# The last layer's K and V projections at the fused stage's beginning, and both masked copies of K written by VectorE

## The reference

```
qn, kn, vn = ln(query), ln(key), ln(value)          # query: L0's output; key = value: the context
Q, K, V = qn @ wq + bq, kn @ wk + bk, vn @ wv + bv   # 16 heads of 8
attn = softmax(Q K^T / sqrt(8));  x = query + (attn V) @ wo + bo
out = x + gelu(ln2(x) @ w1 + b1) @ w2 + b2           # hidden width 512
```

## Time and profile before

| | |
|---|---|
| median of 3 runs | 1389.48 us (1388.59 to 1390.74) |
| the profiled execution, first to last instruction (span) | 1387.9 us; the profile has no other time of its own, and the median stands 1.6 us above |
| mean granted TensorE clock | 0.960 |
| busy share: PE, DVE, ACT, POOL | 89%, 68%, 71%, 65% |
| fused stage, from its first instruction to the MLP's first `up` matmul | 912.2 to 1258.6 us |
| MLP | 1258.6 to the end |
| packets of hardware DMA queues | 23.5% of 16 engines' span |

### The profile page before, as it was taken

How to read it: one execution, slowest core, us unless ns; L and a number is a source line. 1 busy time by engine, 2 the same in 40 slices (tenths; PEclk the granted TensorE clock), 3 DMA queues, 4 the chain that set the end, 5 groups by cost and what they waited for, 6 DMA issues and landing times. The chain is left out here.

```text
span 1387.9 us, 59975 instructions
## 1 busy us (share of the span) xinstructions
PE 1238.4 (89%) x23094; PEld 1036.4 (75%) x23094; DVE 944.3 (68%) x2136; ACT 980.7 (71%) x1956; POOL 897.7 (65%) x1432
## 2 busy tenths in 40 slices
PE   4999999989999998958999999925889998898997
PEld 2778888777788887937999999924677776675775
DVE  3788888877887886595555555525999999864331
ACT  1677787777888887346788776614888888875553
POOL 2577777777777665216999998758677777413431
PEclk9999999999999999579999999966999999999999
DMA  4233434332222320151322222322232333112221
GB/s 126 71 111 110 121 107 127 108 94 87 84 83 83 91 69 26 35 156 39 89 84 81 81 84 66 65 73 69 76 88 82 89 89 91 59 47 61 69 68 46
DMA packets 140285, 113.96 MB, mean 82 GB/s; under 512 B 17184, under 2 KB 113952, under 8 KB 140192
## 3 DMA queue, kind: packets, MB, share of 16 engines
q1 hardware_dynamic: 131744, 95.42, 23.5%
q0 software_dynamic: 8448, 17.32, 5.0%
HBM read 78.55 MB, written 34.08 MB: 81 GB/s over the span
## 5 line engine op out<-in xcount | busy, mean ns | idle before, releaser
L912 DVE TENSOR_REDUCE at_mx<-at_ps_s 128x16 f32<-128x1024 f32 x128 | 156.1, 1220 | 90.4 <-PE at_ps_s L599 46.3
L818 ACT ACTIVATE at_pt<-at_ps_t 128x1024 f32<-128x1024 f32 x128 | 130.6, 1020 | 54.7 <-PE at_ps_t L613 54.0
L811 ACT ACTIVATE at_pr<-at_dd 128x1024 f32<-128x1024 f32 x128 | 135.2, 1056 | 34.6 <-DVE at_dd L920 34.5
L2452 DVE COPY ex_wt<-experts 128x1156 f32 x133 | 102.8, 773 | 82.3 <-DVE ex_y L2458 74.0
L2410 ACT ACTIVATE ex_hg<-ex_ps_h,ex_wt 128x128 f32<-128x128 f32 x544 | 155.1, 375 | 1.2 <-PE ex_ps_y L2369 1.2
L2338 POOL DMA_INDIRECT ex_xg<-x,ex_ti x136 | 139.0, 1022 | 23.4 <-issue 21.8
L920 DVE TENSOR_TENSOR at_dd<-at_ps_s,at_mx 128x1024 f32<-128x1024 f32 x128 | 153.7, 1202 | 0.1
L2360 PE MATMUL ex_ps_h<-ex_xt,ex_wt 128*128 128x128 f32 x1088 | 147.1, 278 | 1.0 <-ACT ex_xt L2402 0.8
L1992 POOL DMA_INDIRECT l_yg<-rows,l_sl x128 | 126.1, 985 | 31.9 <-issue 29.5
L613 PE MATMUL at_ps_t<-ident,at_pr 128*128 128x128 f32 x1024 | 139.3, 279 | 6.1 <-issue 4.2
L2369 PE MATMUL ex_ps_y<-ex_wt,ex_hg 128*128 128x128 f32 x1088 | 143.7, 275 | 0.4 <-ACT ex_hg L2410 0.4
(11 more groups left out here) (262 smaller groups left out, 3154.5 us busy)
## 6 DMA issues: line engine op xcount, KB each, us to landing
rows<-ex_y SPq DMA_DIRECT2D x136, 64.0 KB
x<-at_ln_out SPq DMA_DIRECT2D x32, 256.0 KB, 3.2
at_kx<-in_xt SPq DMA_DIRECT2D x16, 256.0 KB, 2.8
at_qx<-in_xt SPq DMA_DIRECT2D x16, 256.0 KB, 2.8
at_vin<-in_xt SPq DMA_DIRECT2D x16, 256.0 KB, 2.9
at_xr<-in_x SPq DMA_DIRECT2D x16, 256.0 KB, 3.0
cx<-in_ctx SPq DMA_DIRECT2D x16, 256.0 KB, 3.2
x1t<-at_xt SPq DMA_DIRECT2D x16, 256.0 KB, 3.3
```

What stands on the lines that cost most here:

```text
L811: act.activation(pr[:, p], dd[:, p], ACT.Exp, scale=SCALE).then_inc(p_ready, 1)
L818: act.activation(pt[:, 2 * h + p], ps_t[:, :, :, :], ACT.Copy).then_inc(pt_ready, 1)
L912: dve.tensor_reduce(mx[:, p], ps_s[:, :, 4 * p:4 * p + 4, :], AX.X, ALU.max).then_inc(mx_ready, 1)
```

## The change

The context's tile `x2t` lives until the end, and `ctxzt` and its 16 copies go. At the fused stage's beginning PE projects K and V of all 16 groups, each into one of two banks of the score tile `ps_s`. ACT copies K back over the context in `x2t` (`keep_k`); DVE copies V into parts of `pt`, `dd` and `pr` that the loop doesn't use yet (`keep_v`), and SP stores it from there to a DRAM buffer `ctxv`. In the loop PE has no K and V projections any more; SP loads one group of V per step, ACT's `copy_v` reads it from SBUF, and DVE's new `mask_k` writes both masked copies from the kept K, just behind `front_moments`. The 22 matmuls go. The MLP's `hid` and `y` take the place of `dd`.

```diff
 # SP
-                def load_k(a): ...
+                def store_v(g):
+                    sp.wait_ge(vt_ready, g + 1)
+                    sp.dma_start(layer.kv_src[:, bass.ts(g, GT)], staged(g)).then_inc(v_out, 16)
                 def load_v(a):
+                    if a.unrolled and a.g == 0:
+                        sp.wait_ge(v_out, 16 * NG)
                     if beyond(a.g, 0):
-                        sp.wait_ge(v_ready, a.g)
+                        sp.wait_ge(vx_ready, a.g)
 # SP, step: behind load_front
+                    if a.unrolled and -3 <= a.g < 0:
+                        for g in ((0, 1, 2, 3, 4), (5, 6, 7, 8, 9, 10), (11, 12, 13, 14, 15))[a.g + 3]:
+                            store_v(g)
 # PE
+                def project_k(g):
+                    if g > 1:
+                        pe.wait_ge(kt_ready, g - 1)
+                    pe.matmul(bank[g % 2][:, :], layer.wk[:, :], zt[:, bass.ts(g, GT)], ...).then_inc(early_k, 1)
+                def project_v(g):
+                    if g > 1:
+                        pe.wait_ge(vt_ready, g - 1)
+                    ... 16 matmuls into bank[2 + g % 2] as before ...
+                    mm.then_inc(early_v, 1)
 # PE, step
-                        project_k(a.shift(1))
-                        project_v(a)
 # PE, before the steps
-                for k in range(22):
-                    pe.matmul(spare[:, 0:P], c.ident[:, :], c.num[:, 0:P], start=True, stop=True)
+                for g in range(NG):
+                    project_k(g)
+                    project_v(g)
 # ACT
-                def mask_k(a): ... two activations ps_g -> kb ...
+                def keep_k(g):
+                    act.wait_ge(early_k, g + 1)
+                    act.wait_ge(early_v, g + 1)
+                    act.activation(zt[:, bass.ts(g, GT)], bank[g % 2][:, :], ACT.Copy).then_inc(kt_ready, 1)
 # ACT, step: first thing
+                    if a.unrolled and -2 <= g < 0:
+                        for e in ((0, 1, 2, 3, 4, 5, 6, 7), (8, 9, 10, 11, 12, 13, 14, 15))[g + 2]:
+                            keep_k(e)
 # DVE
+                def keep_v(g):
+                    dve.wait_ge(early_v, g + 1)
+                    dve.tensor_copy(staged(g), bank[2 + g % 2][:, :]).then_inc(vt_ready, 1)
+                def mask_k(a):
+                    if a.unrolled and a.g == 0:
+                        dve.wait_ge(kt_ready, NG)
+                        dve.wait_ge(side_ready, 1)
+                    if beyond(a.g, 0):
+                        dve.wait_ge(s_ready, 2 * a.g)
+                    for j in range(2):
+                        ins = dve.tensor_scalar(kb[:, j, :], zt[:, bass.ts(a.place, GT)], c.side[:, 2 + j:3 + j],
+                                                side[:, 0, 2 + j:3 + j], ALU.mult, ALU.add)
+                    ins.then_inc(kb_ready, 1)
 # DVE, step: first thing
+                    if a.unrolled and -3 <= g < -1:
+                        for e in ((0, 1, 2, 3, 4), (9, 10))[g + 3]:
+                            keep_v(e)
 # DVE, step: between front_moments and maximum(2g+2, 0)
+                    if a.shift(1).exists():
+                        mask_k(a.shift(1))
+                    if a.unrolled and -3 <= g < -1:
+                        for e in ((5, 6, 7, 8), (11, 12, 13, 14, 15))[g + 3]:
+                            keep_v(e)
+                    if a.unrolled and g == -1:
+                        dve.wait_ge(v_out, 16 * NG)
 # attention_phase, route_phase, expert_phase
-  ctxzt: 5 + 11 copies x2t -> ctxzt, and the waits for them
```

More of the change, by code:

```diff
@@ L1469, in fused_phase @@
         z4t_ready, qx_ready = n.sem("z4t_ready"), n.sem("qx_ready")
-        in_k, in_v = n.sem("in_k"), n.sem("in_v")
+        in_v, v_out = n.sem("in_v"), n.sem("v_out")
+        early_k, early_v = n.sem("early_k"), n.sem("early_v")
+        kt_ready, vt_ready = n.sem("kt_ready"), n.sem("vt_ready")
         tok_out = [n.sem(f"tok_out{i}") for i in range(2)]
@@ L1481, in fused_phase, with staged @@
         xb_ready, y_ready = n.sem("xb_ready"), n.sem("y_ready")
+        zt = layer.out_tr
+        bank = [ps_s[:, i].rearrange("p a b -> p (a b)") for i in range(4)]
+        def staged(g):
+            whole = (pt.rearrange("p h b r q -> p (h b r q)") if g < NG // 2 else
+                     dd.rearrange("p u r b s -> p (u r b s)") if g < 3 * NG // 4 else
+                     pr.rearrange("p u r b s -> p (u r b s)"))
+            return whole[:, bass.ts(g if g < NG // 2 else g % 4, GT)]
         def held(a):
@@ L1494, in _, with load_v @@
             def _(sp):
[L1495 to L1502 removed]
+                def store_v(g):
+                    sp.wait_ge(vt_ready, g + 1)
+                    sp.dma_start(layer.kv_src[:, bass.ts(g, GT)], staged(g)).then_inc(v_out, 16)
+                def load_v(a):
+                    if a.unrolled and a.g == 0:
+                        sp.wait_ge(v_out, 16 * NG)
+                    if beyond(a.g, 0):
+                        sp.wait_ge(vx_ready, a.g)
                     sp.dma_start(vin[:, :], layer.kv_src[:, bass.ts(a.place, GT)]).then_inc(in_v, 16)
@@ L1541, in scores @@
                         pe.wait_ge(d_ready, 2 * quad)
+                    else:
+                        pe.wait_ge(kt_ready, NG)
+                        pe.wait_ge(vt_ready, NG)
                     for b in range(QB):
@@ L1596, in widen @@
                               stop=True).then_inc(r_ready, 1)
[L1598 to L1601, removed]
+                def project_k(g):
+                    if g > 1:
+                        pe.wait_ge(kt_ready, g - 1)
+                    pe.matmul(bank[g % 2][:, :], layer.wk[:, :], zt[:, bass.ts(g, GT)], start=True, stop=True).then_inc(
+                        early_k, 1)
                 def project_q(a):
@@ L1613, in project_v @@
                         for j in range(2):
-                            mm = pe.matmul(ps_g[64 * j:64 * j + 64, t:t + SEQ], vin[:, t:t + SEQ],
-                                           w[:, :, j, :], start=True, stop=True)
-                    mm.then_inc(v_ready, 1)
+                            mm = pe.matmul(bank[2 + g % 2][64 * j:64 * j + 64, t:t + SEQ],
+                                           zt[:, GT * g + t:GT * g + t + SEQ], w[:, :, j, :], start=True, stop=True)
+                    mm.then_inc(early_v, 1)
                 def project_out(a):
@@ L1719, in copy_v @@
                         dst = c.vx[half, 0].rearrange("p b r (a m) -> p (b r) a m", a=2)[:, :, :, 16 * j:16 * j + 8]
-                        src = ps_g[half, :].rearrange("p (w a m) -> p w a m", a=2, m=8)
+                        src = vin[half, :].rearrange("p (w a m) -> p w a m", a=2, m=8)
                         ins = act.activation(dst, src, ACT.Copy)
@@ L1797, in step @@
                         copy_o(g * 2 - 1, 1)
-                    if a.shift(1).exists():
-                        mask_k(a.shift(1))
                     if a.exists():
@@ L2316, in step @@
                     sp.dma_start(out_rows[bass.ts(i, P), :], y[:, s, :]).then_inc(y_out[s], 16)
-                    if s == TU - 1 and turning:
-                        sp.dma_start(ct_out[:, bass.ts(q + NCT, GT)], xt_ctx[:, bass.ts(q + NCT, GT)]).then_inc(zc_stored, 16)
                 over_tiles(sp, step)
@@ L2479, in build @@
     x4 = scratch("x4", (T, D))
-    ctxzt = scratch("ctxzt", (D, T))
+    ctxv = scratch("ctxv", (P, T))
     rows = scratch("rows", (NT * P, D))
@@ L2504, in build @@
                 Layer(c, "sa", d["xt"], d["xt"], d["x"], x1, x1t, True, c.row["ln1_g"], c.row["ln1_b"], False, False),
-                Layer(c, "ca", x1t, d["ctxt"], x1, x2, x2t, False, c.row["ln2_g"], c.row["ln2_b"], False, True, True)], d["ctx"], ctxzt, late)
+                Layer(c, "ca", x1t, d["ctxt"], x1, x2, x2t, False, c.row["ln2_g"], c.row["ln2_b"], False, True, True)], d["ctx"], late)
             r.experts = m.sb("experts", [P, E, W])
@@ L2510, in build @@
             experts = ctx.enter_context(ExitStack())
-            done = expert_phase(nc, c, r, "ex_", x2, rows, x2t, ctxzt, done, experts)
+            done = expert_phase(nc, c, r, "ex_", x2, rows, x2t, done, experts)
             routing.close()
         fused_phase(nc, c, r, "l1_",
-                    Layer(c, "l1", None, ctxzt, x2, x4, None, False, None, None, True, False), x2, rows,
+                    Layer(c, "l1", None, ctxv, x2, x4, x2t, False, None, None, True, False), x2, rows,
                     (d["l1_w1"], d["l1_b1"], d["l1_w2"], c.row["l1_b2"], out), done)
```

52 lines of the change are left out of this document (14 added, 38 removed).

## The result

The changed kernel takes 1441.9 us (1440.2 to 1442.6) beside 1390.1 us of the kernel before on the same chip: 1.0371 times as long, 95% interval 1.0352 to 1.0390. The forecast was 1420.5, with a range up to 1441: the direction was right, the size was 21 us short.

A forecast was written before the change was run, and what follows sets the result against it. A ring through several engines, no engine full, was taken to set the 18.09 us step. Twelve steps at 2.3 us more gave 28, light steps +1, beginning +2: 1389.5 + 31 = 1420.5 us, range 1399 to 1441.

The forecast's parts named there:

- the ring: Fused loop: mask, scores, turn, copy, scales, `exponent`, `recip` in series set the step, 19.5 us against 18.09 before.
- Mask and handover: Start of the loop's new series: VectorE's two masked copies, 0.88 us, then a handover of 0.06 to the scores.
- the clock's price: Loop: TensorE's pause lowers its clock, adding 0.92 us per step through the scores; bounds 0 and 1.5.
- about 3 us: Loop: how long the low clock was expected to last in every step.
- the turn's 0.6: Loop: possible loss of the turn behind the scores at the low clock, about 0.6 us, not counted.
- the light steps: Steps 13 to 15: lose projections on PE, gain mask and scores on VectorE; +1 us, between -2 and +4.
- the beginning: Start of the fused stage: early projections and `keep_v` delay the first steps, +2 us.
- rival of a slow beginning: Beginning stays at the low clock or waits for its V: 1420.5 plus 10 to 30, so 1440; chance 0.07.
- GpSimd's root first: Loop: second masked copy waits for GpSimd's power instruction, 2 us more per step, 1444 us; chance 0.11.
- The clock holds: Loop: TensorE's clock stays at 1.00, steps of 19.5 us, 1409.5 us in all; chance 0.21.
- VectorE alone: Loop: VectorE's work alone sets the step, 18.1 us, no more than before; 1386 us; chance 0.11.

The follow-up runs named there:

- early_mask: Changed kernel with both masked copies of K moved on VectorE from behind `front_moments` to ahead of the second `recip`: 1395.0 us, 1.0042.
- kb_two: Changed kernel with the masked copies at the same place, but double-buffered and written one group ahead: 1408.7 us, 1.0130.
- fill4: Changed kernel with four extra unused matmuls of 128x512 on TensorE while it waits for the masked copies: 1416.4 us, 1.0174.
- both_first: Changed kernel with masked copies on ScalarE, `weigh_second` ahead of the second `recip`, and `subtract` ahead of `normalise`: 1391.1 us, 1.0011.
- all_dve: Changed kernel, masked copies ahead of `weigh_second`, reordered as both_first, GpSimd's `shift_own` ahead of its next fetches and the second `spread`: 1397.3 us, 1.0048.

## Why the prediction was wrong in size

*Right: what is on the ring.* Each link that the prediction named is in the timeline in its order. Mask and handover took 1.10 us (forecast 0.94); at full clock the step is 19.6 (forecast 19.5). early_mask shows that the place of the copies, and not their work, is what the change costs. kb_two adds what the prediction left out: with the copies at that place and nobody waiting for them, 0.9 us per step is left at full clock, through `subtract` and the second scores, through GpSimd's root, or both.

*Wrong: the size of the clock's price.* The failed step is "As the fall comes at no fixed point of the pause, I take the scores' share alone, 0.92: a step of 20.4 us". What it left out, the turn's 0.6, is there in the step shown (1.67 against 1.06). Nor does the low stretch last "about 3 us" in every step: four of the twelve have 3.4 us of it, the others 5.8 to 7.7 (in the second window shown from 1173.5 to 1180.3, well past the turn). The one fall that the "about 3 us" was read from began at 983.2 by its own row (0.61 over 983 to 984), not at 983.6, and lasted 3.4 us. Measured 1.7 to 1.9 us per step, over the upper bound of 1.5 and about 0.9 more than forecast: 11 of the missing 21 us.

*Wrong: the light steps.* "I take +1, between -2 and +4" became +10.1. The interval from step 12 to 13 alone is 19.94 against 16.12; it takes 15.97 in early_mask, 17.67 in kb_two and 19.29 in fill4 (3.4 us of it at the low clock). So the ring through mask and scores binds there as well, and the pauses of VectorE that were to cover it do not lie behind the copies. From step 12 to the MLP's first `up` matmul, the light steps and what leads over to the MLP, it was 63.3 us before and 72.4 after: these are the other 9 us. early_mask takes 64.1, kb_two 66.9 and fill4 69.0, but kernels without the wait and with VectorE's order changed also reach 69.1 (both_first), so only the first interval is told apart by cause.

*Right: the beginning.* +1.9 us in the span, 1.0 of it behind the expert stage; forecast +2. TensorE's clock was up after two projections (pairs of 2.14 us from 917.99 on). The rival of a slow beginning (1440) gave nearly the measured time, by a cause that is not there.

*The rivals.* GpSimd's root first (1444) was as near the measured time and as wrong: both copies take 0.97 us in the step shown, and it is GpSimd that is held up beside them:

```profile
1152.19 0.41 POOL L2034 TENSOR_TENSOR l_fneg<-l_fmv,minus_one 128x8 f32<-128x8 f32 x1 [0.80 <-DVE l_fmv L1925]
1152.57 0.49 POOL L2035 TENSOR_TENSOR l_frstd<-l_fmv,eps 128x8 f32<-128x8 f32 x1
1153.14 1.68 POOL L2038 TENSOR_TENSOR l_frstd<-l_frstd,minus_half 128x8 f32<-128x8 f32 x1
```

The two small ones take 0.41 and 0.49 us, 0.20 each in both_first, where no copy lies beside them; the power instruction starts when the copies are done, and here the root still ends before ScalarE needs it (in kb_two it does not). The Trainium skill, SBUF — State Buffer, section Who interferes with whom, says of such a copy that whichever of the two engines issues first keeps the shared ports; these rows agree. "The clock holds" is what fill4 builds: 1416.4, against 1409.5 by the forecast. VectorE alone comes near to setting a step only in all_dve.

## What to carry to other kernels

An instruction that takes work off two engines can still make a step longer: follow what is queued right behind it, on its own engine and on the one that waits for it, and look for a pause of the same engine that lies before the consumer needs the result. Here the same two copies cost 0.2 us per step in a pause and 3.4 at the place where they were put. Price a new TensorE pause with all the work of the ring that runs behind it at the low clock, in light steps as well.

## What the runs showed of the hardware

One pause per step was enough to bring TensorE's clock down each time where it lasted 4.5 us (67.4 us at the low level in twelve steps), in six of twelve steps where it lasted 1.9 (20.5 us), and in none where it lasted 1.0 to 1.3 (0.1 us): four matmuls per step whose result nobody reads bought 25 us. I had not expected that equal pauses would be followed by 3.4 us at the low level in one step and by twice as much in the next, nor that in single profiles of fourteen kernels a stage that is the same in all of them would end 904.8 to 911.4 us into the span.
